# Second layer of a two-layer token kernel: outer convolution taps as four wide operations, V moved by ScalarE

## What is computed

```python
def _L1_attn_ref(x, c_attn_w, c_attn_b, c_proj_w, c_proj_b):
    qkv = x @ c_attn_w + c_attn_b
    q, k, v = jnp.split(qkv, 3, axis=-1)
    ...
    out = jnp.einsum('bhqk,bhkd->bhqd', weights, v)
    out = out.transpose(0, 2, 1, 3).reshape(B, T, D)
    return out @ c_proj_w + c_proj_b

def _L1_ffn_ref(x, w1, conv_w, conv_b, w2):
    h = bit_linear(x, w1)
    h = depthwise_conv1d(h.transpose(0, 2, 1), conv_w, conv_b)
    h = h.transpose(0, 2, 1)
    h = jax.nn.silu(h)
    return bit_linear(h, w2)
```

## Time and profile before

| | us |
|---|---|
| median of three runs | 1017.11 (1012.09 to 1017.53) |
| the profiled execution, time | 1011.83 |
| its span in the trace | 1010.0 |
| PE / DVE / ACT / POOL busy | 827.3 / 657.0 / 435.8 / 423.6 |
| TensorE clock granted, mean | 0.914 of full speed |

### The profile page before, as it was taken

The page is one execution under the profiler, slowest core; times in us unless marked ns, Lnnn a source line. Parts: engine busy times, 40 slices in busy tenths (PEclk is TensorE's granted clock), DMA queues, the critical chain, the costliest instruction groups (busy, mean ns, idle before and its releaser), DMA issues.

```text
span 1010.0 us, 20955 instructions
## 1 busy us (share of the span) xinstructions
PE 827.3 (82%) x7141; PEld 719.5 (71%) x7141; DVE 657.0 (65%) x1810; ACT 435.8 (43%) x1032; POOL 423.6 (42%) x717
## 2 busy tenths in 40 slices
PE   2999999999999882599966978888888888888842
PEld 2888888888888771366646867777777777777731
DVE  0255666766667545322212589899999998899974
ACT  0244343443434422122213456656556565556551
POOL 0243444544445422433316655554544555554100
PEclk9999999999999965699997999999999999999866
DMA  5336420100000221122210000000000000000000
GB/s 150 91 99 182 149 49 8 20 14 8 8 6 10 71 71 37 28 66 69 67 41 8 12 7 12 13 12 10 10 13 13 7 13 13 13 13 7 7 7 11
DMA packets 23911, 36.50 MB, mean 36 GB/s; under 512 B 9896, under 2 KB 21138, under 8 KB 23042
## 3 DMA queue, kind: packets, MB, share of 16 engines
q1 hardware_dynamic: 14402, 26.27, 9.4%
q0 software_dynamic: 5808, 5.63, 2.6%
q10 hardware_dynamic: 3600, 3.28, 0.9%
HBM read 27.28 MB, written 7.88 MB: 35 GB/s over the span
## 4 chain that ended last, share of the span: by engine, by line
PE 40%; DVE 26%; POOL 11%; ACT 8%; issue 7%; DMA 5%; SPq 2%; DVEq 0%; ACTq 0%; POOLq 0%
PE bank_h L1204 6%; PE bank_a L1223 4%; PE bank_b L1232 3%; PE bank_c L1241 3%; POOL base L530 3%; DVE stats L815 3%; DVE w L1024 3%; DMA h<-in_txt 3%; DVE diff L808 3%; PE bank_g L1186 2%; PE bank_e L1359 2%; PE bank_c L1375 2%; DVE spare L280 2%; DVE rowmax L805 2%; PE bank_f L1359 2%
## 5 line engine op out<-in xcount | busy, mean ns | idle before, releaser
L455 POOL TENSOR_TENSOR qbd<-qt,consts_f 128x560 f32<-128x560 f32 x128 | 146.6, 1156 | 222.5 <-PE bank_e L1176 181.9
L572 ACT ACTIVATE pt<-bank_g 69x448 f32<-69x448 f32 x128 | 69.7, 544 | 108.3 <-PE bank_h L1186 108.3
L1186 PE MATMUL bank_g<-consts_f,prob 112*69 112x112 f32 x512 | 74.6, 269 | 46.7 <-ACT prob L567 46.5
L463 POOL TENSOR_TENSOR veps<-mv,consts_f 69x2 f32<-69x2 f32 x64 | 25.1, 393 | 192.4 <-DVE mv L820 191.7
L567 ACT ACTIVATE prob<-diff 112x345 f32<-112x345 f32 x128 | 62.6, 489 | 93.5 <-DVE diff L808 93.5
L1204 PEld LDWEIGHTS bank_h<-values,pt 69*69 69x69 f32 x1024 | 80.7, 157 | 21.4 <-ACT pt L572 18.9
L1204 PE MATMUL bank_h<-values,pt 69*69 69x68 f32 x1024 | 83.4, 240 | 15.0 <-ACT pt L572 12.9
L1186 PEld LDWEIGHTS bank_g<-consts_f,prob 112*69 112x69 f32 x512 | 53.9, 144 | 55.8 <-ACT prob L567 53.7
L1204 PE MATMUL bank_d<-values,pt 69*69 69x68 f32 x1024 | 73.6, 229 | 0.0
L1176 PEld LDWEIGHTS bank_e<-kt,qbd 128*112 128x112 f32 x640 | 72.0, 180 | 0.3
L1176 PEld LDWEIGHTS bank_f<-kt,qbd 128*112 128x112 f32 x640 | 72.1, 180 | 0.0
(11 more groups left out here) (199 smaller groups left out, 1984.6 us busy)
## 6 DMA issues: line engine op xcount, KB each, us to landing
w<-in_w SPq DMA_DIRECT2D x2, 4096.0 KB, 16.4
patches<-in_patches SPq DMA_DIRECT2D x16, 222.0 KB, 2.6
expert_results<-prob ACTq DMA_DIRECT2D x25, 128.0 KB, 2.0
expert_rows<-x SPq DMA_DIRECT2D x16, 138.0 KB
out<-h SPq DMA_DIRECT2D x16, 138.0 KB
f_raw<-in_f SPq DMA_DIRECT2D x2, 1024.0 KB, 8.1
patches<-in_b SPq DMA_DIRECT2D x1, 2048.0 KB, 10.8
wqkv<-in_wqkv SPq DMA_DIRECT2D x2, 768.0 KB
```

The costliest lines, as they stand in the source:

```text
L455: pool.tensor_tensor(qbd[u % 2][:], q.broadcast_to([128, NG, HPB, QG]), head_mask.unsqueeze(1).unsqueeze(3).broadcast_to([128, NG, HPB, QG ...
L572: act.activation(pt[u % 2][:, :, 0:4, :].rearrange("t h g q -> t g h q"), banks["g"][0:T, 0:4 * SR].rearrange("t (g h q) -> t g h q", g=4, ...
L1186: ins = nc.tensor.transpose(banks[bank][0:T, at * SR:(at + 1) * SR], prob[u % 2][:, g, :], ident[0:SR, 0:SR])
```

## The change

In layer 2 the sixteen `outer_taps` operations per pair become two wide multiplications (`multiply_tap`, into new tiles) and two wide additions (`add_tap`). V is moved by ACT without its bias, at the head of the next step. The bias goes once through the projection and is added to the output bias. The placeholders and index copies are gone in both layers: the operation itself holds the wait, and a gather reads its indices from the large table. The output rows' store waits for the count of bank b's reads.

```diff
+            def move_v(S, BK, p):
+                act.wait_ge(S["v_made"], p + 1)
+                wait(act, S["attended"], UNITS * p)
+                act.activation(vv[:, :, :, 0:DH], banks["b"][0:T, :].rearrange("t (b h d) -> t b h d", b=2, h=H),
+                               ACT.Copy).then_inc(BK["b"], 1)
...
             def body1(s):
+                if live(s, 1, PAIRS):
+                    move_v(S, BK, s - 1)
                 if live(s, 2, PAIRS):
                     move_ot(S, BK, s - 2, 1)
...
-                    wait(act, F["conv_next"], HFC * (p + 1))
+                    wait(act, F["conv_added"], 2 * (p + 1))
...
-                carry_wait(dve)
                 for b in range(2):
                     ins = dve.bn_stats(stats[:, which, b, :], src(p, b))
                 ins.then_inc(S["ln_chain"], 1)
                 dve.wait_ge(S["ln_chain"], ln_count)
-                carry_wait(dve)
...
+            dve.tensor_tensor(v_rows1[:], v_bias1[:].unsqueeze(2).broadcast_to([128, KC, T]),
+                              ones[:, 0:T].unsqueeze(1).broadcast_to([128, KC, T]), ALU.mult).then_inc(v_rows_made, 1)
...
+            dve.wait_ge(v_rows_projected, 1)
+            dve.tensor_tensor(o_bias1[:], banks["e"][0:T, 0:D], o_bias1[:], ALU.add).then_inc(o_bias_made, 1)
...
-            def outer_taps(p, g):
-
-                for j in range(*GROUPS[g]):
-                    dve.wait_ge(F["conv_mid"], HFC * p + j + 1)
-                    dve.scalar_tensor_tensor(yc[:, j, :, 1:T], hs[:, j, :, 0:T - 1], conv[:, j, 0:1],
-                                             yc[:, j, :, 1:T], ALU.mult, ALU.add).then_inc(F["conv_prev"], 1)
...
+            def multiply_tap(p, side, lag):
+
+                for g, bank in enumerate(HIDDEN_BANKS):
+                    dve.wait_ge(BK[bank], reads(p + lag, order[bank], f"hidden{g}", done=True))
+                wait(dve, F["conv_added"], 2 * p)
+                weight = lambda k: conv[:, :, k:k + 1].unsqueeze(3).broadcast_to([128, HFC, 2, T - 1])
+                if side == 0:
+                    dve.tensor_tensor(taps[0][:, :, :, 1:T], hs[:, :, :, 0:T - 1], weight(0), ALU.mult).then_inc(F["taps_made"], 1)
+                else:
+                    dve.tensor_tensor(taps[1][:, :, :, 0:T - 1], hs[:, :, :, 1:T], weight(2), ALU.mult).then_inc(F["taps_made"], 1)
+
+            def add_tap(p, side):
+
+                dve.wait_ge(F["taps_made"], 2 * p + side + 1)
+                dve.wait_ge(F["conv_mid"], HFC * (p + 1))
+                wait(dve, F["conv_added"], 2 * p + side)
+                at = slice(1, T) if side == 0 else slice(0, T - 1)
+                dve.tensor_tensor(yc[:, :, :, at], yc[:, :, :, at], taps[side][:, :, :, at], ALU.add).then_inc(F["conv_added"], 1)
...
-                    outer_taps(s - 3, 1)
+                    multiply_tap(s - 3, 0, 2)
...
-                    dve.wait_ge(BK["b"], reads(s, order["b"], "ffn_out", done=True))
-                    carry_wait(dve).then_inc(F["out_ready"], 1)
...
-                    outer_taps(s - 3, 2)
+                    multiply_tap(s - 3, 1, 2)
...
-                    outer_taps(s - 3, 3)
+                    add_tap(s - 3, 0)
+                    add_tap(s - 3, 1)
...
-                if live(s, 0, PAIRS):
-                    move_v(S, BK, s, 1)
-                if live(s, 2, PAIRS):
-                    outer_taps(s - 2, 0)
...
-                carry_wait(pool)
-                pool.tensor_copy(yidx[:], yrow_i[:, bass.ds(2 * p, 2)]).then_inc(yidx_made, 1)
-                wait(pool, yidx_made, p + 1)
-                carry_wait(pool)
                 for b in range(2):
-                    pool.indirect_dma_start(yg[:, b, :], None, results, bass.IndirectOffsetOnAxis(yidx[:, b:b + 1], 0)
+                    pool.indirect_dma_start(yg[:, b, :], None, results, bass.IndirectOffsetOnAxis(yrow_i[:, 2 * p + b:2 * p + b + 1], 0)
                                             ).then_inc(y_gathered, 16)
...
+            pe.wait_ge(v_rows_made, 1)
+            for c in range(KC):
+                ins = mm(banks["e"][0:T, 0:D], v_rows1[:, c, :], wo1[:, c, :], start=c == 0, stop=c == KC - 1)
+            ins.then_inc(v_rows_projected, 1)
```

More of the change, by code:

```diff
@@ L256, in program @@
         hs, yc, z = cut(0), cut(1), cut(2)
+        taps = [cut(4), cut(5)]
         zb = ffn[:, 3 * NW:3 * NW + NW // 2].bitcast(BF16).rearrange("p (j b t) -> p j b t", j=HFC, b=2)
@@ L270, in program @@
         zmax = sb("zmax", [128, 2, T])
-        spare = sb("spare", [1, 384], BF16)
-        spare_at = {}
-        def carry_wait(eng):
-            first = 0 if eng is nc.gpsimd else 192
-            at = spare_at[first] = (spare_at.get(first, 0) + 1) % 192
-            return eng.tensor_tensor(spare[:, first + at:first + at + 1], ones[0:1, 0:1], ones[0:1, 0:1], ALU.mult)
         consts_in = sem("consts_in")
@@ L336, in program @@
         bias_added = sem("bias_added")
-        FN = ("quant_chain quantized diag1_made spread1_made hidden_made conv_mid conv_prev conv_next tanh_made "
-              "z_made zmax_made max_turned diag2_chain spread2_made z_rounded z_int ffn_made out_ready out_stored").split()
+        v_rows_made = sem("v_rows_made")
+        v_rows_projected = sem("v_rows_projected")
+        o_bias_made = sem("o_bias_made")
+        FN = ("quant_chain quantized diag1_made spread1_made hidden_made conv_mid taps_made conv_added tanh_made "
+              "z_made zmax_made max_turned diag2_chain spread2_made z_rounded z_int ffn_made out_stored").split()
         F = {n: sem(f"ffn_{n}") for n in FN}
@@ L426, in store_rows @@
             def store_rows(p):
-                sp.wait_ge(F["out_ready"], p + 1)
+                sp.wait_ge(BS[1]["b"], reads(p + dict(BANKS1["b"])["ffn_out"], BANKS1["b"], "ffn_out", done=True))
                 sp.dma_start(out[bass.ds(2 * p, 2)].rearrange("b t d -> t b d"),
                              h[:, bass.ds(2 * p, 2), :]).then_inc(F["out_stored"], 16)
-            with sp.Fori(0, PAIRS) as p:
+            for p in range(PAIRS):
                 store_rows(p)
@@ L504, in gather @@
                         wait(pool, tile_turned, 2 * s + k - 1)
-                        carry_wait(pool)
-                        pool.tensor_copy(gidx[:, k:k + 1], tile_tokens[:, bass.ds(2 * s + k, 1)]).then_inc(gidx_made, 1)
-                        wait(pool, gidx_made, 2 * s + k + 1)
-                        carry_wait(pool)
-                        pool.indirect_dma_start(xg[k], None, rows, bass.IndirectOffsetOnAxis(gidx[:, k:k + 1], 0)
+                        pool.indirect_dma_start(xg[k], None, rows, bass.IndirectOffsetOnAxis(tile_tokens[:, 2 * s + k:2 * s + k + 1], 0)
                                                 ).then_inc(gathered[k], 16)
@@ L1018, in scale_hidden @@
                     s1b[:].unsqueeze(1).broadcast_to([128, j1 - j0, 2, T]), ALU.mult).then_inc(BK[bank], 1)
-            def outer_taps(p, g):
-                for j in range(*GROUPS[g]):
-                    dve.wait_ge(F["conv_mid"], HFC * p + j + 1)
-                    dve.scalar_tensor_tensor(yc[:, j, :, 1:T], hs[:, j, :, 0:T - 1], conv[:, j, 0:1],
-                                             yc[:, j, :, 1:T], ALU.mult, ALU.add).then_inc(F["conv_prev"], 1)
-                for j in range(*GROUPS[g]):
-                    dve.wait_ge(F["conv_prev"], HFC * p + j + 1)
-                    dve.scalar_tensor_tensor(yc[:, j, :, 0:T - 1], hs[:, j, :, 1:T], conv[:, j, 2:3],
-                                             yc[:, j, :, 0:T - 1], ALU.mult, ALU.add).then_inc(F["conv_next"], 1)
+            def multiply_tap(p, side, lag):
[13 more added lines that the diff above has]
+                dve.tensor_tensor(yc[:, :, :, at], yc[:, :, :, at], taps[side][:, :, :, at], ALU.add).then_inc(F["conv_added"], 1)
             NORMS = (("x", 0), ("x2", 2))
```

33 lines of the change are left out of this document (12 added, 21 removed).

## The result

| | before | after |
|---|---|---|
| median of four runs each | 1015.55 us | 1031.09 us |
| all runs | 1012.09 to 1017.53 | 1028.71 to 1037.17 |
| profiled execution, its span | 1011.83, 1010.0 | 1028.71, 1026.9 |
| mean granted TensorE clock | 0.914 | 0.896 |
| first zmax, last zmax | 597.82, 992.69 | 588.01, 1009.99 |

The ratio is 1.0166, with a 95% interval of 1.011 to 1.0222: slower by 1.7%, where 1.0% was forecast. The time lies in the range of 1012 to 1038 and 4 us above the forecast of 1027.

The account below looks back on a forecast made before the run. Waits in layer 2's steps bound it, on late ACT work, then a POOL chain held by DVE, not the busiest engine. +20.8 there and -10.3 for placeholders gave +10.5; on the median 1017.11, forecast 1027 us, range 1012 to 1038.

Parts of the forecast that it names:

- the late product: Layer 2, first half of a step: PE's product into bank b waits for ACT's V copy, +2.0 us on PE, +0.93 a step.
- up to the first zmax: Layer 1 and start of layer 2, before the first large maximum over z: removed placeholders and copies give -10.3 us.
- steps 4 to 15: Layer 2's twelve repeating steps: 0.93 in the first half plus 0.4 in the second, each, +16.0 us.
- Step 16: Layer 2, the step without new gathers, running on DVE alone: 0.93 + 1.4, +2.3 us.
- steps 17 and 18: Layer 2's last steps: both adds and a multiply stand behind the residual, +1.25 us each.
- T to R: Step's first half, from PE turning the maxima to DVE starting unit 1's row maximum: 13.84 us before, +0.93 forecast.
- It ends at 806.8: Layer 2: PE's product into bank b, delayed from 802.91 to 804.9, was to end at 806.8.
- R to z: Step's second half, from unit 1's row maximum on DVE to z's start: 8.78 us before, 10.13 forecast.
- Rival B: Layer 2: POOL beats z and its bias add of 1.26 holds DVE each step; 1037 us, chance 0.15.
- worth nothing: Layer 2, DVE: sixteen small outer taps and four wide operations both take 4.9 us, so no gain on DVE.
- Rival D: DVE's load decides and small operations cost what they last: -1 us a step, about 1000 us, chance 0.10.
- A: Layer 2: the late product is partly hidden, so steps 4 to 15 stay at 27.35; 1011.6 us, chance 0.13.

Follow-up runs that it names:

- run 6: The kernel before without GpSimd's index copy and its two placeholders ahead of the second layer's gathers: 1012.68 us, ratio 0.9981.
- run 4: The changed kernel with ACT's copy of V put earlier, in the step that made V, ahead of the last middle taps; wide taps stay: 1010.00 us.
- run 5: The changed kernel with ACT's copy of V at the early place and the small outer taps back: 981.72 us, ratio 0.9687.
- 9 and 10: Unit 2's attention product done three times on PE ahead of T, in the changed kernel and in the kernel before: 1030.35 and 1024.09 us.
- run 1: The changed kernel with V moved by DVE again at its old place; wide taps stay: 1009.53 us, ratio 0.9958.
- run 3: The changed kernel with V on DVE and the small taps back; folded bias and missing placeholders and index copies stay: 988.69 us, ratio 0.9738.
- run 7: run 3 with DVE's placeholder between the residual add and the row maximum of unit 1 put back: 1006.61 us, ratio 0.9912.
- run 8: run 3 with POOL's two placeholders and index copy ahead of the second layer's gathers put back: 998.58 us, ratio 0.9849.

## Why the prediction was right, and where its terms were not

The forecast's direction, its range and its largest term, the late product, were right; that the single halves came so near their numbers was in part luck.

| term | forecast | measured |
|---|---|---|
| up to the first zmax | -10.3 (with all placeholders) | -9.8 |
| steps 4 to 15 | +16.0 | +20.6 |
| step 16 | +2.3 | +4.2 |
| steps 17 and 18 | +2.5 | +2.3, then -0.4 to the end |
| sum | +10.5 | +16.9 (medians +15.5) |

**The first layer.** -9.8 against -10.3 is closer than a single pair of traces can tell, since kernels with the same first layer spread over 7 us (above). The kernel before also has four first-layer steps of 21.8 to 21.9 in its trace, 3.3 us in all over the usual 21.04, which run 6's trace lacks. From one common step to the next the gain is 0.31, not the 0.4 of the sum.

**The late product.** Right in place and size: V's copy starts 1.57 behind the four taps' start, the product 2.3 behind it where it used to be 0.3, DVE idles 1.36 before its residual add. Run 4 shows that it is this wait: the early copy alone brings T to R from 15.09 to 13.48. T to R was forecast at 14.77; it is 15.03 and 15.17 in turn in the earlier steps, 14.88 and 15.35 in the later ones.

**The missing 0.3 a step.** The sentence that failed is "It ends at 806.8": the product's 1.91 was carried over. In every other step it takes up to 3.00, at the lower clock. The wait of 1.84 for V goes ahead of it there, but in the later steps it does so ahead of the fast ones too; it is needed (with V early, in run 4, the product takes 1.91 in every step, as it does before the change) and not enough. T to R is 15.09 on the mean and not 14.77: 12 x 0.32 = 3.9 of the 4.6 us by which steps 4 to 15 were under-forecast. No term of the sum was for the clock, though the trace of before shows the key projection at 2.08 behind a gap of 2.35. The sum carried that over, inside the 13.84 from T to R; runs 5, 9 and 10 show the projection at 1.12.

**The second half.** R to z was forecast as 10.13 and is 10.19 to 10.20 in eleven of twelve steps; z won the race against POOL's multiply, and the second normalisation starts 11.6 after R, as said (11.7). Up to there the steps were right. The rest is luck: T was to come 13.9 after R and came at 13.72 and 14.10 in turn, 13.94 on the mean. The 0.38 between them is PE's turning of the probabilities at the lower clock, which no term held. Rival B (GpSimd's bias add holds z) did not come about.

**Step 16.** Forecast +2.3, measured +4.2. The second half gave 1.55 of it, near the 1.4 of the sum. The first half grew by 2.7, and not by the 0.93 of the late product, which didn't wait there at all. PE's clock was down instead, 0.50 from 940 to 944 and 0.52 from 944 to 950, where the kernel before had 0.57 from 929 to 933 and 1.00 from 933 to 939.

**The outer taps "worth nothing".** DVE's busy time was indeed no gain to speak of (the three wide groups of a step take 2.02, 1.28 and 2.71, 6.0 in all with the first held by POOL, against 4.9 forecast). On the time it does not stand up: the wide form costs 20.8 us (run 1 less run 3) or 28.3 (run 4 less run 5). In the sum I had 1.55 for the adds' place, less what the placeholders gave back. The Trainium skill's advice, "VectorE: DVE Perf Modes", section on the TRN2 errata, of wide tiles to pay the fixed latency less often would have it the other way round; sixteen small fused operations that start 0.27 apart beat four wide ones here. The wide ones need a pass for the product and a pass for the sum, and a gather beside the adds takes 2.34; which of the two costs more wasn't tried. The prediction cited the section "The DRAIN you can't avoid" of the same page of the Trainium skill in half: it also says that a next operation that is not held starts earlier. The trace agrees with that part, 0.27 between the starts of two operations, the second of which ends 0.35 after its start. Rival D's direction (the wide form as a gain) is refuted, and so is A: the product's delay was not hidden, the period grew.

**The placeholders.** Near in the total, wrong in the makeup. I gave them -10.3 outside the second layer's steps and, inside, 0.72 before R and 4 x 0.08 behind it, together 1.04 a step and so about -23 in all. Run 3 has -24.5. But its period is 1.44 shorter, not 1.04, and its first layer gave less (its last two steps were long, at a clock of 0.55 from 338 to 352 us). And what VectorE's placeholder costs isn't its duration: run 7's lasts 0.57 in most steps, 12 x 0.57 = 6.8 us, and costs 17.9. The sentence "the gathers start without copies but their descriptor work runs into the second add" held for the changed kernel. With the small taps the missing copies are worth 9.9 us (run 8) and in the kernel before, alone, 2 us that can't be told from none (run 6): their worth hangs on where the power then falls. In the wide form they weren't put back.

**The bias fold** I put at 0; no run changes it alone, so this wasn't tried.

## What to carry to other kernels

Before an operation is moved to an idler engine, ask who waits for the buffer that it reads: here a 0.58 us copy, put behind 1.67 us of taps, held a product for 2 us, and the same copy ahead of those taps held it for 0.27. Where two engines exclude each other from a port, the order in which they arrive is worth more than either operation, and removing tiny operations pays or not by the side on which it lets the next one fall (9.9 us in run 8, 2 in run 6); test the parts of a change one by one, since 42 us of loss and 25 of gain showed here as a plain 1.7%. And an idle gap on TensorE can have a second price behind it: read the granted clock in the stretch after a gap before taking a matmul's duration as fixed.

## What the runs showed of the hardware

- Behind a gap on TensorE of 2.41 us the granted clock was 0.71 and 0.56 in the two stretches that follow, and eight matmuls of 140 columns took 2.08 instead of 1.12 us. They took 1.53 to 2.08 behind every gap of 1.9 to 2.6 us in the second layer's full steps, and behind gaps of 0.8 to 1.1 in some steps and not in others.
- Filling such a gap with repeated work brings the clock back in most steps (26.75 and 27.93 a step instead of 27.4 and 29.1), and costs more than it gives where the clock falls all the same (5.67 us for what takes 3.19).
- A GpSimd gather took 2.33 to 2.34 beside a wide VectorE add and 1.18 to 1.29 without; a GpSimd power of 69x2 elements 1.80 to 1.97 beside z and 0.70 to 0.72 without. In run 5 the bias add met z and took 2.41 to 2.43 instead of 1.27; PE's turn followed the maximum all the same.
